# Turning the x block on TensorE in ten steps of sixteen instead of two, and the orders of work that go with it

## The reference

```
proj = x @ in_proj_w.T                      # gate, hBC, dt
hBC  = silu(causal_conv4(hBC) + conv_b)     # hs: 128 heads x 64; B, C: 8 groups x 128
dt   = softplus(dt + dt_bias);  A = -exp(A_log)
per chunk of 128 tokens and head:
  xch    = hs * dt                          # tokens x 64
  Y_diag = (C B^T * L) xch                  # L = exp of differences of cumsum(dt*A)
  state  = decay*state + (B*decay)^T xch;   Y_off = exp(A_cum) * C state_before
Y = Y_diag + Y_off + hs*D
g = Y * silu(gate);  normalise over each group of 1024;  * norm_w;  @ out_proj_w.T
x = layernorm(x + that);  x = layernorm(x + x @ (W + LoRA).T + bias)
```

## Time and profile before

| | |
|---|---|
| median of 3 runs | 1569.7 us (1568.87 to 1572.33) |
| the profiled execution's own time | 1572.33 us |
| its span in the profile | 1570.5 us |
| busy: PE, DVE, ACT, POOL | 1540.6, 1354.5, 1209.6, 1335.6 us |
| mean granted clock of TensorE | 0.996 |

### The profile page before, as it was taken

One profiled execution on the slowest core, in us unless ns is written; L12 is line 12 of the kernel. 1 busy time (PEld: TensorE's weight loads), 2 busy tenths in 40 slices (PEclk: granted clock), 3 DMA queues, 4 the chain that ended last, 5 costly groups with the idle time before them and its releaser, 6 DMA issues.

```text
span 1570.5 us, 27374 instructions
## 1 busy us (share of the span) xinstructions
PE 1540.6 (98%) x8664; PEld 1259.0 (80%) x8664; DVE 1354.5 (86%) x1878; ACT 1209.6 (77%) x2360; POOL 1335.6 (85%) x1124
## 2 busy tenths in 40 slices
PE   8999999999999999999999999999999999999998
PEld 6878888887888878888788878888888887888765
DVE  6778898888989799897989889897898879988797
ACT  5888778886878877887877877878777886778864
POOL 4489789897998979998899988999799897999974
PEclk9999999999999999999999999999999999999999
DMA  3655444544454443545355444454435445364431
GB/s 118 214 184 162 158 123 150 168 143 130 128 175 155 125 151 126 181 135 152 125 154 162 131 148 135 139 179 141 134 128 172 151 122 157 115 189 141 166 104 61
DMA packets 164190, 229.04 MB, mean 146 GB/s; under 512 B 25040, under 2 KB 86480, under 8 KB 163792
## 3 DMA queue, kind: packets, MB, share of 16 engines
q1 hardware_dynamic: 163040, 227.14, 46.4%
q10 hardware_dynamic: 1008, 0.17, 0.1%
HBM read 193.14 MB, written 34.08 MB: 145 GB/s over the span
## 4 chain that ended last, share of the span: by engine, by line
PE 59%; POOL 16%; issue 9%; DVE 8%; ACT 5%; DMA 2%; ACTq 0%; SPq 0%; POOLq 0%; DVEq 0%
PE proj L560 10%; PE proj L562 10%; PE proj L561 10%; PE p_out L608 5%; PE p_out L610 5%; PE p_out L609 5%; PE p_yd L736 5%; PE p_st L617 4%; POOL w_lo L1080 2%; POOL xd L1116 2%; POOL dh L1160 2%; DMA raw<-w_t 2%; POOL xd_lo L1120 2%; ACT decay L890 2%; DVE bT L1276 2%
## 5 line engine op out<-in xcount | busy, mean ns | idle before, releaser
L560 PE MATMUL proj<-x_hi,w_hi 128*128 128x512 f32 x1160 | 463.6, 400 | 9.2 <-DVE x_lo L1410 6.9
L562 PE MATMUL proj<-x_hi,w_lo 128*128 128x512 f32 x1160 | 453.8, 391 | 0.0
L561 PE MATMUL proj<-x_lo,w_hi 128*128 128x512 f32 x1160 | 453.7, 391 | 0.0
L890 ACT ACTIVATE decay<-decay,tok 128x128 f32<-128x128 f32 x1024 | 312.6, 391 | 0.0
L1276 DVE SCALAR_TENSOR_TENSOR hs<-proj,uch,hs 128x511 f32<-128x511 f32 (+2 forms) x384 | 283.5, 738 | 29.3 <-ACT hs L829 24.2
L1080 POOL TENSOR_TENSOR w_lo<-raw,w_hi 128x512 fp32r<-128x512 f32 x177 | 251.4, 1420 | 40.1 <-ACT w_hi L802 33.2
L560 PEld LDWEIGHTS proj<-x_hi,w_hi 128*128 128x128 f32 x1160 | 219.4, 189 | 53.8 <-issue 8.8
L562 PEld LDWEIGHTS proj<-x_hi,w_lo 128*128 128x128 f32 x1160 | 218.7, 189 | 46.3
L561 PEld LDWEIGHTS proj<-x_lo,w_hi 128*128 128x128 f32 x1160 | 219.4, 189 | 42.1
L1314 DVE TENSOR_TENSOR decay<-decay,cb 128x1024 f32<-128x1024 f32 x128 | 209.8, 1639 | 46.5 <-ACT decay L908 46.4
L1160 POOL TENSOR_TENSOR dh<-dh,eac 128x512 f32<-128x512 f32 x96 | 131.0, 1365 | 99.2 <-DVE eac L1345 96.6
(11 more groups left out here) (143 smaller groups left out, 3024.3 us busy)
## 6 DMA issues: line engine op xcount, KB each, us to landing
decay<-acum_d SPq DMA_DIRECT2D x128, 512.0 KB, 4.4
raw<-w_t SPq DMA_DIRECT2D x177, 256.0 KB, 2.8
turned_d<-x_blk SPq DMA_DIRECT2D x112, 256.0 KB, 2.0
x_tok_sb<-turned_d SPq DMA_DIRECT2D x448, 64.0 KB, 1.9
eac<-eacum_d SPq DMA_DIRECT2D x192, 128.0 KB, 3.1
wo_raw<-wo_t SPq DMA_DIRECT2D x32, 256.0 KB, 3.5
c_new<-wo_t SPq DMA_DIRECT2D x32, 256.0 KB, 4.3
hs<-x_t SPq DMA_DIRECT2D x8, 256.0 KB, 5.3
```

What stands on the lines that cost most here:

```text
L560: nc.tensor.matmul(dst[:], w_hi[:, ws, k, :], x_hi[:, k, cols], start=(k == 0), stop=False)
L561: nc.tensor.matmul(dst[:], w_hi[:, ws, k, :], x_lo[:, k, cols], start=False, stop=False)
L562: mm = nc.tensor.matmul(dst[:], w_lo[:, ws, k, :], x_hi[:, k, cols], start=False, stop=(k == KC - 1))
L890: ins = nc.scalar.activation(decay[:, dslot(c), h, :], decay[:, dslot(c), h, :], ACT.Relu, scale=-1.0, bias=tok[:, e, 0, c, h:h + 1])
```

## The change

It turns ten steps of a group on PE: c = 0, (0, 1), (0, 7) and all of unit 1 but (1, 1). Six steps are still turned through DRAM; in four of them, (0, 2), (0, 3), (0, 5), (1, 1), DVE multiplies by dt, in two, (0, 4) and (0, 6), POOL does. The places of some other work change: the second projection of step (0, 6), the early mix in (1, 3), POOL's order in (1, 1) and (0, 6), `add_normed`, and the sum of squares of (0, 0).

```diff
-MIXED_FIRST = (3,)
-WEIGHT_FIRST = ((1, 1),)
+BY_DVE = frozenset([(0, 2), (0, 3), (0, 5), (1, 1)])
+BY_POOL = frozenset([(0, 4), (0, 6)])
+TURNED = sorted(BY_DVE | BY_POOL)
...
         def turn_n(g, e, c):
-            return 7 * (2 * g + e) + c
+            return g * len(TURNED) + (TURNED.index((e, c)) + 1)
+        def turn_at(g, e, c, last):
+            o, te, tc = ahead(e, c, 2)
+            return (g + o, te, tc) if (te, tc) in TURNED and not (last and o) else None
...  # SP
-            store_blocks(0, 0, 1)
-            load_blocks(0, 0, 1)
...
-                        if c2 and not (last and o2):
-                            store_blocks(g + o2, e2, c2)
+                        turned = turn_at(g, e, c, last)
+                        if turned:
+                            store_blocks(*turned)
...  # PE, front
-                if c == 0:
+                if (e, c) not in TURNED:
                     wait(pe, xdt_ready, step(g, e, c))
-                    pe.wait_ge(hs_ready, 8 * u + (7 if u else 4))
+                    if c == 0 or c == CPB:
+                        pe.wait_ge(hs_ready, 8 * u + (8 if c else 7 if u else 4))
                     for j in range(UT):
                         mm = nc.tensor.transpose(...)
...  # PE, step
-                        if (e, c) == (0, 6):
-                            project(g, todo.pop(0))
...  # POOL
-                        if (e, c) in WEIGHT_FIRST and tiles and splits[0]:
-                            split_lo(g + splits[0][0], splits[0][1])
-                            splits[0] = None
...
-                                if c < 7 and (e, c) != (0, 6):
-                                    scale_tokens(g, e, c + 1)
+                                if (ne, ncn) in BY_POOL:
+                                    scale_tokens(g + off, ne, ncn)
                                 gate_y(g, e, c)
-                                if (e, c) == (0, 6):
-                                    scale_tokens(g, e, 7)
                                 lagged_rms(g, e, c)
-                                if (e, c) == (1, 1) and splits[1]:
-                                    split_lo(g + splits[1][0], splits[1][1])
-                                    splits[1] = None
...  # DVE, front
+                if (e, c) in BY_DVE:
+                    dve.wait_ge(x_here, 64 * turn_n(g, e, c))
+                    dve.wait_ge(dt_blk_ready, 2 * (2 * g + e + 1))
+                    wait(dve, xd_scaled, carried(g, e, c))
+                    nc.vector.tensor_tensor(xdt..., x_tok_sb[...], bcast(dt_blk[:, c], 3, BLK), ALU.mult)
+                elif (e, c) not in TURNED:
+                    dve.wait_ge(hid_ready, hid_n(g, e, c))
                     wait(dve, xd_scaled, carried(g, e, c))
                     nc.vector.tensor_tensor(xdt[:], p_hid[:], bcast(tok[:, e, 1, c, :], 2, HD), ALU.mult)
...  # DVE, step
-            turn_blocks(0, 0, 1)
...
-                        if e == 1 and c in MIXED_FIRST:
-                            mix(g, 1, c + 1)
...
-                        if e == 1 and c > 2 and not last:
-                            add_normed(g, c - 3)
...
-                        if c2 and not (last and o2):
-                            turn_blocks(g + o2, e2, c2)
+                        if turned:
+                            turn_blocks(*turned)
...
-                        if more and not (e == 1 and c in MIXED_FIRST):
+                        if more:
                             mix(g + off, ne, ncn)
...
-                        if last and e == 1 and c > 1:
+                        if e == 1 and c > 1 and (c < 7 or last):
                             add_normed(g, c - 2)
...
-                        late_sum = (e, c) == (0, 0) and g > 0
-                        if e == 0 and not late_sum:
+                        if e == 0:
                             wait(dve, var_ready, 8 * g - 7 + c)
                             nc.vector.tensor_reduce(sqs[:, c, :], sq_view, AX.X, ALU.add).then_inc(sqs_ready, 1)
```

More of the change, by code:

```diff
@@ L274, in turn_n, with hid_n @@
         def turn_n(g, e, c):
-            return 7 * (2 * g + e) + c
+            return g * len(TURNED) + (TURNED.index((e, c)) + 1)
+        def hid_n(g, e, c):
+            return g * (16 - len(TURNED)) + sum(1 for k in range(8 * e + c + 1) if (k // 8, k % 8) not in TURNED)
+        def turn_at(g, e, c, last):
+            o, te, tc = ahead(e, c, 2)
+            return (g + o, te, tc) if (te, tc) in TURNED and not (last and o) else None
         def weight_n(g, t):
@@ L509, in body @@
                             load_decay(sp, g + od, ed, cd)
-                        o2, e2, c2 = ahead(e, c, 2)
-                        if c2 and not (last and o2):
-                            store_blocks(g + o2, e2, c2)
+                        turned = turn_at(g, e, c, last)
+                        if turned:
+                            store_blocks(*turned)
                         tiles = tiles_of(e, c, last)
@@ L517, in body @@
                                 load_tile(g + off, LOOP_TILES[n], last)
-                            if i == 0 and c2 and not (last and o2):
-                                load_blocks(g + o2, e2, c2)
-                        if not tiles and c2 and not (last and o2):
-                            load_blocks(g + o2, e2, c2)
+                            if i == 0 and turned:
+                                load_blocks(*turned)
+                        if not tiles and turned:
+                            load_blocks(*turned)
                         if g == 0 and e == 0:
@@ L1103, in scale_tokens @@
                 pool.wait_ge(yd_ready, step(g, e, c))
-                if c == 1:
-                    pool.wait_ge(dt_blk_ready, 2 * (2 * g + e + 1))
+                pool.wait_ge(dt_blk_ready, 2 * (2 * g + e + 1))
                 nc.gpsimd.tensor_tensor(xdt[:].rearrange("p h d -> p (h d)").rearrange("p (j i b) -> p i j b", j=UT, i=UT),
@@ L1150, in body @@
                         off, ne, ncn = after(e, c)
-                        tiles = tiles_of(e, c, last)
-                        splits = [split_after(e, c, i, last) for i in range(len(tiles))]
-                        if (e, c) in WEIGHT_FIRST and tiles and splits[0]:
-                            split_lo(g + splits[0][0], splits[0][1])
-                            splits[0] = None
                         if c % CPB:
@@ L1167, in body @@
                             rstd_of(0, c - 3)
+                        tiles = tiles_of(e, c, last)
                         for i, t in enumerate(tiles):
-                            if splits[i]:
-                                split_lo(g + splits[i][0], splits[i][1])
+                            nxt = split_after(e, c, i, last)
+                            if nxt:
+                                split_lo(g + nxt[0], nxt[1])
                             if i == 0 and (g, e, c) == (0, 0, 0):
-                                scale_tokens(0, 0, 1)
                                 decay_hidden(0, 0, 1)
@@ L1191, in body @@
                         if not tiles:
-                            if c < 7:
-                                scale_tokens(g, e, c + 1)
-                            else:
+                            if (ne, ncn) in BY_POOL:
+                                scale_tokens(g + off, ne, ncn)
+                            if c == 7:
                                 lagged_rms(g, e, c)
@@ L1284, in front @@
             def front(g, e, c):
-                if c == 0:
-                    dve.wait_ge(hid_ready, 2 * g + e + 1)
+                if (e, c) in BY_DVE:
+                    dve.wait_ge(x_here, 64 * turn_n(g, e, c))
+                    dve.wait_ge(dt_blk_ready, 2 * (2 * g + e + 1))
+                    wait(dve, xd_scaled, carried(g, e, c))
+                    nc.vector.tensor_tensor(xdt[:].rearrange("p h d -> p (h d)").rearrange("p (j i b) -> p i j b", j=UT, i=UT),
+                                            x_tok_sb[:, turn_n(g, e, c) % 2], bcast(dt_blk[:, c], 3, BLK), ALU.mult).then_inc(xdt_ready, 1)
+                elif (e, c) not in TURNED:
+                    dve.wait_ge(hid_ready, hid_n(g, e, c))
                     wait(dve, xd_scaled, carried(g, e, c))
@@ L1516, in body @@
                         sq_view = ysq[:].rearrange("p a b -> p b a")
-                        late_sum = (e, c) == (0, 0) and g > 0
-                        if e == 0 and not late_sum:
+                        if e == 0:
                             wait(dve, var_ready, 8 * g - 7 + c)
                             nc.vector.tensor_reduce(sqs[:, c, :], sq_view, AX.X, ALU.add).then_inc(sqs_ready, 1)
-                        elif late_sum:
-                            pass
                         elif last:
@@ L1553, in body @@
                                 wo_split_lo(g, e, (0, 1) if e else (0,))
-                        if late_sum:
-                            wait(dve, var_ready, 8 * g - 7)
```

(1 more changed line is left out.)

1 line of the change is left out of this document (removed).

## The result

The changed kernel takes 1586.9 us (median of 4 runs, 1585.3 to 1587.3) against 1569.5 of the kernel before (median of 4, 1568.9 to 1572.3). The ratio is 1.0105, with a 95% interval of 1.0093 to 1.0116. So it is slower by 17.4 us. The forecast was 1597, with a range of 1583 to 1614: the sign and the range held, and the size was 10 us too large, 27 for 17. The profiled execution took 1586.3, its span 1584.5, which is 14.0 more than the 1570.5 of before.

What follows compares the result with a forecast made beforehand. The prediction took PE's instruction stream as the bound, so added transposes are paid unless they fall into waits. Its terms, 26 - 5.7 - 2.7 + 10.8 + 2.8 - 4 = +27.2 us on 1569.7, gave 1597, range 1583 to 1614.

Steps and rivals of the forecast that it cites:

- PE's transposes, +26: Eight more steps a group turned on PE, 64 sets at 0.39 to 0.42 us, paid in full: +26 us.
- Four passes: Rival: each PE transpose costs 0.23 us, as a single-pass matmul of 512 does; 1630 us, chance 0.02.
- The wait of (1, 4), -5.7: PE's 0.82 us wait for POOL's xd_lo in (1, 4) vanishes in 7 groups: -5.7 us.
- The wait of (1, 2), -2.7: PE's 0.45 us wait for the state in (1, 2) shrinks by 0.39 in 7 groups: -2.7 us.
- The new wait of (0, 6), +10.8: Without the early second projection, PE waits 1.35 us for xd_lo before L748 in (0, 6), 8 times: +10.8 us.
- DVE has 0.7 us more in (0, 4), of which I let 0.4 through: Part of the (0, 6) wait: DVE's added work in (0, 4) delays the eac starting POOL's chain, by 0.4 us.
- w_lo late in (1, 1), +2.8: POOL makes dh and the state before w_lo in (1, 1), so PE waits 0.4 us in 7 groups: +2.8 us.
- DVE, 0: DVE gains 3.4 us a group from exchanging turnings for multiplies, mostly in unit 0's idle time: nothing on the path.
- Start and end, -4: Group 0's wait for xd_lo goes, with some clock loss (-3); last group's wait for g_lo shrinks (-1).
- DMA, 0: 64 stores and 256 loads fewer, taken as nothing; at most 2.4 us of POOL's waits for x_tok_sb come back.
- the waits go and none comes: Rival: PE's old waits go and xd_lo in (0, 6) comes sooner, so +14 us, 1584; chance 0.15.
- DVE or POOL takes over: Rival: DVE's two-SBUF-operand multiplies collide with POOL, delaying xd_lo and L748, 3 us a group: 1610 to 1622; chance 0.18.

Runs made afterwards that it cites:

- e5: Changed kernel's turning and multiply split, with all orders of work as in the kernel before; 1576.6 us, ratio 1.0033 to the kernel before.
- e1: Changed kernel with each set of four PE transposes made twice (c = 0 excepted); 1603.3 us, ratio 1.0202 to the kernel before.
- e11: Changed kernel with POOL instead of DVE multiplying in (0, 2), (0, 3), (0, 5), (1, 1); 1591.1 us, ratio 1.0126 to the kernel before.
- e3: Changed kernel with only w_lo put back before dh in (1, 1); 1582.4 us, ratio 1.0071 to the kernel before.
- e9: Kernel before, its orders kept, with only (1, 2) to (1, 5) turned on PE besides c = 0; 1568.2 us, ratio 0.9981.
- e7: Kernel before with one more step, (1, 4), turned on PE and nothing else; 1574.0 us, ratio 1.0022.
- e2: Changed kernel with only the second projection of (0, 6) put back before L748; 1581.1 us, ratio 1.0065 to the kernel before.
- e8: Kernel before, no sets added on PE, with DVE instead of POOL making 12 of the 14 multiplies; 1592.7 us, ratio 1.0145.
- e6: Kernel before, its turning kept and POOL multiplying in 14 steps, with only the orders of the change; 1605.0 us, ratio 1.022.
- e12: Kernel before with (1, 4) also turned on PE and `add_normed` moved behind the state update; 1578.3 us, ratio 1.0051.

## Why the prediction was right, and 10 us too large

By its own steps, in the order of the sum:

- *PE's transposes, +26.* Right. A step with a set grows by 0.37 to 0.41 (e5 has no wait beside it), 64 x 0.375 = 24, and e1 shows that PE's stream pays. The term was 2 too large, because I took the value between 0.39 and 0.42 of (0, 7); the sets of unit 1 cost 0.37. "Four passes" is refuted: that would have been 0.92 a set.
- *The wait of (1, 4), -5.7.* Right in size: its step is 3.2 us shorter over groups 0 to 6 with seven sets more, so 5.8 of waiting are gone. In e5 it is more, 1.08 a group: the step held more than the 0.82 that the timeline names, and the orders of the change keep 0.25 of it.
- *The wait of (1, 2), -2.7.* The mechanism was right and the size too small: 2.2 us shorter with seven sets more, so 4.8. The step held 0.76 us of waiting (e5), and the timeline names 0.45 of it; I had priced less than the named part.
- *The new wait of (0, 6), +10.8.* This is the step that failed: the wait came, at L748's matmul, for POOL's xd_lo, but it is 0.6 us and not 1.35; e5, which takes it away, is shorter there by 0.57 to 0.61 (0.73 in group 0), 4.9 in all. The part "DVE has 0.7 us more in (0, 4), of which I let 0.4 through" had the wrong sign. POOL's dh, which DVE's eac releases, starts 11.25 us behind the p_yd of (0, 4) in the kernel before and 10.81 behind it in the changed one: 0.44 *sooner*. e11 shows the cause: with POOL making the multiplies, dh starts at 11.26 again and (0, 6) is 0.43 longer. DVE's mix of (0, 4) is 0.76 us shorter when POOL has no multiply ahead of its xd, and a wait of 0.30 for ACT goes; together that outweighs the multiply of 0.75 us that DVE gained.
- *w_lo late in (1, 1), +2.8.* The wait came, but that the number is near is luck. It is 0.61 to 0.65 a group (e3), 4.4 in all and not 2.8. Over groups 0 to 6 (1, 1) grows by only 4.8, of which the sets are 2.8 (0.40 each there), because 2.4 us of an old wait in this step went that I hadn't seen (e5).
- *DVE, 0.* On the path it is nothing, as said, though the multiply's price was wrong: 1.355 us, for 0.9 taken, and outside the bound of 1.17 that POOL's row gave. The bound was wrong because the multiply's time isn't its own: it starts while POOL gates y (31 of 32 times), and in all 32 cases it takes what is left of POOL's instruction and 0.55 us more. DVE's gain a group was forecast at 3.4 us and is 166.91 - 164.60 = 2.3, since its other instructions shrank.
- *Start and end, -4.* Too small. The first p_yd comes 0.5 sooner, (0, 1), (0, 2) and (1, 2) of group 0 are 1.5 shorter, the end 1.3, and group 7, which has its sets and the wait of (0, 6) like the others, grows by 0.4 and not by 3.6. That is some 6.5. In group 7, 2.8 us are the lower clock of the profiled execution of before, of which waits in (1, 4) give 1.5 and more back; the rest is a shorter wait for g_lo (1.59 for 2.56) and a step (1, 6) that is 0.96 shorter. The clock's part belongs at least partly to that one execution: three executions of before have a mean clock as low as 0.996 here, and each is the slowest of its series (1572.3, 1572.7, 1572.9).
- *DMA, 0.* A term is missing here, of some 2.4 us. The wait for x_tok_sb, the one I looked at, was 2.4 us in all for POOL and is 0.6 for DVE now. But the late load of a weight in (1, 1) had cost PE 2.4 us over groups 0 to 6, and the changed kernel doesn't have that wait. Whether fewer DMAs take it away or the 0.40 us that PE's new set puts into that step is open: in e9, with ten of the DMA turns left and that set, it is gone too, and in e7, with 13 turns and no set there, it isn't.

For the profiled execution, 27.2 were forecast and 14.0 came by the spans. Of the 13.2 between, 5.9 are the wait of (0, 6), 2.5 start and end (with the clock in group 7), 2.1 the wait of (1, 2), some 2 the sets, and 0.8 (1, 1), where 1.6 too little for w_lo and 2.4 for the weight's load nearly cancel. The forecast was made against the median, from which this profiled execution of before stands 2.8 above; that is why 10 of the 13 are seen in the medians.

The rivals: "the waits go and none comes" gave 1584, closer to 1587 than the forecast is, yet by another way, for both new waits came (e2, e3). The number is near because they are small and the old ones were larger. "DVE or POOL takes over" did not happen in the changed kernel; e8 and e6 show that it lies close: with 12 multiplies a group on DVE, or with 14 on POOL and these orders, PE idles for 3.7 and 4.8 us in a group. What it said of collisions is true in its sign: the multiply of DVE with two SBUF operands is 1.355 where POOL is beside it. The Trainium skill's "SBUF — State Buffer", section "Who interferes with whom", says that such a DVE operation and a GpSimd one shut each other out for a whole instruction. The trace agrees, both ways. In (0, 2) of group 3 of the changed kernel:

```profile
664.87 1.28 POOL L1220 TENSOR_TENSOR y<-y,gate 128x512 f32<-128x512 f32 x1
665.01 1.69 DVE L1288 TENSOR_TENSOR xdt<-x_tok_sb,dt_blk 128x512 f32<-128x512 f32 x1
666.12 1.48 POOL L1134 TENSOR_TENSOR dh<-hs,uch 128x512 f32<-128x512 f32 x1
```

When the multiply starts, 1.14 us of POOL's y are left, and it takes 1.14 + 0.55. POOL's dh starts with 0.58 of the multiply left, and takes 0.58 + 0.90 where it takes 1.04 with nothing beside it. So what a multiply costs POOL is what was left of it, less 0.14, and not an instruction each.

What is shown and what is argued: that the orders cost most of the difference (9.7 us by the spans, some 11 by the ratios), and that the two new waits are 9 us of it, is shown (e2, e3, e5). Which of the other orders keeps 0.25 us in (1, 4) is open. That the sets cost 24 is shown by the starts and by e1. Why DVE's mix in (0, 4) got shorter is shown by e11 and the rows beside it. That the relief of PE in (1, 2) to (1, 5) needs both POOL's multiplies gone and a longer PE stream is argued from e7, e8 and e9 together: DVE is also less busy there in e9 (45.99 us for 47.04), and no run relieves POOL without giving PE or DVE more to do.

## What to carry to other kernels

An engine at 98% with a second one at 99% of a stretch is bound by both: the wait that the profile names there is only the last to end, and taking it away uncovers one of equal size for the other engine, as 0.82 us for xd_lo became 0.91 us for the state. Work can be moved to the busiest engine for nothing in just those steps where it waits, and costs its full price in each other: four sets at the right steps came out 0.2% below the kernel before, all eight (with four multiplies on DVE, e5) 0.3% above. An engine's instruction can also be priced by what it waits for on another engine: here giving DVE one multiply more made its chain shorter. And an order written by hand belongs to the load it was made for: changing it cost some 10 us under one split of the work and 32 us under another, so a change of who does what and a change of when are to be timed apart.

## What the runs showed of the hardware

- DVE's multiply of 128x512 fp32 with both operands in SBUF takes 0.75 to 1.77 us, mean 1.355 for 32 of them, and 0.993 for the 96 of e8 (0.67 to 1.77); the form that reads PSUM takes 0.678 to 0.686. All 32 start while an instruction of POOL is under way, and take what is left of it and 0.54 to 0.55 us. The same instruction on POOL took 1.17 with 112 in the run and 1.05 with 16.
- The mix of DVE does the same: where POOL's y, dh, xd or w_lo is under way when it starts, it takes what is left of that and 1.08 to 1.09 us (117 of 118 such cases in the kernel before), and 1.20 to 1.23 with POOL idle. g_lo takes what is left and 0.55, and 0.68 alone. So their means follow POOL's load: the mix went from 1639 to 1445 ns, g_lo from 1024 to 910. One `add_normed` took 0.74 us in its old place and 1.32 in a new one (e12).
- The other way round, POOL's dh that starts during such an instruction takes what is left of it and 0.90 us, 1.04 alone; its xd the same, 0.90 and 1.04.
- Behind a wait of 2.56 us PE stood at a granted clock of 0.50, and 17 matmuls took 6.10 us there, 3.27 at 1.00.
- A transpose of 128 fp32 columns starts every 0.11 us in a row of eight (785.75 - 784.90 = 0.85 us for eight in e1), a float32r matmul of 512 columns every 0.23.
